# First loads of layer 0 in four pieces, and 79 expert blocks instead of 80, in a two-layer transformer kernel

## The chip, the cores and the metric

One core of a Trainium2 chip runs the whole program. The metric is the device time of one execution in microseconds (us). All data are float32, apart from a few constants and parked values in bfloat16.

## What is computed

Two layers work on x, 2048 tokens of 512 features, in sequences as each step takes them. Every step is added to x and followed by a layer norm:

```python
x = _layernorm(x + _L0_attn_ref(...))    # linear attention, 16 heads of 128, 4 key/value heads, rope, elu + 1
x = _layernorm(x + _L0_xattn_ref(...))   # mLSTM with the context, 16 heads of 32
x = _layernorm(x + _L0_ffn_ref(...))     # silu, silu, rows added by a top-2 router
x = _layernorm(x + _L1_attn_ref(...))    # lightning attention
x = _layernorm(x + _L1_xattn_ref(...))   # softmax attention with the context
x = _layernorm(x + _L1_ffn_ref(...))     # mixture of experts
```

The two places of the change are the first step and the last. The first begins with `k = x @ Wk.T`, with Wk of 512 x 512. The last sends each token to 4 of 16 experts, chosen inside the best 2 of 4 groups; an expert is `silu(x @ W1.T) * (x @ W3.T) @ W2.T` with 352 inner features, its result is weighted by the router's score, and a shared expert with 704 inner features takes every token.

## The kernel before, in words

The program is written engine by engine: SP issues loads and stores, PE multiplies, DVE and ACT evict PSUM banks and do the element-wise work, POOL adds, and issues the indirect transfers. Semaphores (`wait_ge`, `then_inc`) tie them together. Three parts follow each other: `build_layer0` (tiles named a_), `build_layer1` (c_) and `build_experts` (d_).

**Layer 0** takes the 2048 tokens in four groups of 512 (`stages`). A written list (`order`) assigns the products of a group to the 8 PSUM banks in turn: `Tiles.start` lets PE wait until the bank's earlier tile is drained, `Tiles.done` announces the new one. A group begins with four key tiles (L761, `keys`), one for each key head, 128 x 512, each the sum over four 128-row chunks `c` of the features: `w[:, c, ...]` by `xT[:, c, :]`. A float32 product of one chunk stands in the profile as two MATMUL records. Four value tiles follow, then the query tiles of the first heads, then scores. Weights come through a ring of two 1 MB buffers (`ring`, filled by `fill` at L404 in the order of `RING`): keys in buffer 0, values in 1, first queries in 0 again. For the rope DVE makes two partial products of each key or query tile (L994, L997), POOL adds them (L507), ACT takes the exponential (L545, L547), and DVE writes the feature (L1007). The partial buffers are double, so tile n waits for tile n - 2.

At the start SP issues, in this order, xT of group 0 (1 MB, L410), the key weights (1 MB, L404), cos, sin and the identity (64 KB each, L423) and the value weights (L404). ACT's queue carries nine smaller loads beside them (L533, L535). Before its first product PE waits at L733 for cos, sin and the identity together (`weights`, 48) and for nine constants that POOL writes.

**The experts.** A first phase transposes x, runs the router, ranks the chosen pairs, gives each expert as many blocks of 128 rows as it needs, and scatters the token numbers into a slot list in memory (64 indirect DMAs of POOL, L2246), while PE works on the shared expert for groups 0 and 1 (L2336, L2349). The number of blocks is fixed when the program is built: `BLOCKS = TOKENS * TOPK // P + NE`, 64 + 16 = 80. Blocks past the last needed one run with the last expert on rows that nobody reads.

The loop (`Fori(0, BLOCKS // 2)`, two blocks in each turn, buffers v = 0 and 1) runs on every engine. For block j, PE transposes the gathered rows of block j + 1 (`turn`, L2385), makes the gate products of j (`up_rows`, L2395), transposes the hidden rows of j - 1 (`turn_hidden`, L2390), makes the up products of j (L2395) and the down products of j - 1 (`down`, L2402). DVE copies the transposed rows (L2593), the transposed hidden rows (L2596) and multiplies gate by up (L2612); ACT takes silu of the gate (L2323) and copies the down result (L2316); SP stores it (L2219) and fetches the next expert's weights when the owner changes; POOL gathers the rows of j + 1 (L2258). `filled` counts five steps of PE for each block. Behind the loop the down products of the last block are made and stored, then the shared expert runs on groups 2 and 3, while POOL fetches the result rows back (L2274) and DVE adds them, weighted, to y.

## Time and profile before

| | us |
|---|---|
| median of three timed runs | 2944.35 |
| lowest, highest | 2939.48, 2947.29 |
| the profiled execution | 2941.02 |
| its span | 2939.2 |
| PE busy in the span | 2685.3 (91%) |
| DVE, ACT, POOL busy | 1372.6, 839.4, 588.4 |

The span goes from the first to the last instruction that the profiler recorded; the 1.8 us between it and the execution's time lie around it. All rows below are from this one execution. Times in them are counted from the start of the span. PE stands for TensorE's matmuls, PEld for its weight loads, DVE for VectorE, ACT for ScalarE, POOL for GpSimd and SP for SyncE; L745 is line 745 of the kernel, and where a helper issues the instruction it is the helper's line. "issue" is idle time for which the profile shows no releaser.

### The profile page before, as it was taken

The page shows a single profiled execution, that of the slowest core. Times are in us where ns is not written, and L with a number is a line of the kernel's source. Part 1 is how long each engine was busy: PE and PEld are TensorE (multiplying, and loading weights), DVE is VectorE, ACT ScalarE, POOL GpSimd, SP SyncE. Part 2 cuts the span into 40 slices and gives each one's busy share as a digit, 9 for nine tenths or more (in the row PEclk, how much of TensorE's full clock was granted, in tenths as well). Part 3 has the DMA queues.
Part 4 walks back from the last instruction along what each step waited for, and adds up shares of the span by engine and source line. Part 5 has one row for each costly group of instructions (what it writes and reads, how often), then busy time and mean ns, then how long its engine had stood idle before and what let it go on. Part 6 is the DMA issues. An engine that isn't in the chain of part 4 may idle for free. (4 is left out here: it accounts for less than half of the span.)

```text
span 2939.2 us, 33813 instructions
## 1 busy us (share of the span) xinstructions
PE 2685.3 (91%) x10989; PEld 1366.4 (46%) x10990; DVE 1372.6 (47%) x2541; ACT 839.4 (29%) x1894; POOL 588.4 (20%) x632
## 2 busy tenths in 40 slices
PE   7998999999999856799999999769599999999998
PEld 3544554554455342344334433153256555666543
DVE  3555554563557263467777777423012222222255
ACT  2324332432343231145545555510001111111101
POOL 2111101110111000322333223004311111111154
PEclk9999999999999878899999999969699999999999
DMA  5120122122102103435545454240113333342144
GB/s 189 58 72 29 58 72 86 58 83 76 57 29 72 43 1 127 76 72 116 101 106 111 108 105 102 61 163 1 35 57 129 129 128 130 105 154 97 63 140 154
DMA packets 110236, 261.00 MB, mean 89 GB/s; under 512 B 21955, under 2 KB 55619, under 8 KB 98211
## 3 DMA queue, kind: packets, MB, share of 16 engines
q1 hardware_dynamic: 95202, 220.27, 25.3%
q0 software_dynamic: 13648, 38.06, 4.4%
q8 instruction: 71, 1.16, 0.2%
q10 hardware_dynamic: 1264, 1.10, 0.1%
q14 instruction: 51, 0.41, 0.1%
HBM read 203.76 MB, written 55.22 MB: 88 GB/s over the span
## 5 line engine op out<-in xcount | busy, mean ns | idle before, releaser
L2395 PE MATMUL d_bank<-d_w,d_xcol 128*128 x1280 | 407.0, 461 | 0.0
L1957 DVE TENSOR_REDUCE c_mx<-c_pair 128x2 f32<-128x1024 f32 x256 | 303.6, 1217 | 110.5 <-PE c_pair L1818 109.5
L1668 ACT ACTIVATE c_probs<-c_exp 128x512 f32<-128x512 f32 x512 | 277.9, 597 | 218.4 <-PE c_exp L1832 215.3
L745 PE MATMUL a_bank<-a_xT,a_ring 128*128 128x512 f32 x640 | 287.3, 600 | 11.2 <-DMA a_ident<-in_ident 11.2
L507 POOL TENSOR_TENSOR a_ry<-a_rt 128x512 f32<-128x512 f32 x80 | 131.4, 1642 | 790.9 <-DVE a_rt L997 790.9
L2395 PEld LDWEIGHTS d_bank<-d_w,d_xcol 128*128 128x128 f32 x1280 | 231.8, 191 | 102.4 <-issue 1.5
L2402 PE MATMUL d_bank<-d_w,d_hid 128*128 (+1 forms) x486 | 221.9, 592 | 0.6 <-DVE d_hid L2596 0.6
L745 PE MATMUL a_bank<-a_wo,a_ot 128*128 128x512 f32 x512 | 222.4, 592 | 0.0
L2336 PE MATMUL d_bank<-d_xT,d_ws 128*128 128x512 f32 (+1 forms) x384 | 179.4, 620 | 34.9 <-issue 34.2
L745 PEld LDWEIGHTS a_bank<-a_xT,a_ring 128*128 128x128 f32 x640 | 120.8, 193 | 150.6 <-issue 137.2
L1832 PE MATMUL c_exp<-c_qs,c_ks 128*128 128x512 bf16 x512 | 160.3, 384 | 16.0 <-ACT c_probs L1668 7.6
L2316 ACT ACTIVATE d_yrow<-d_bank 128x512 f32<-128x512 f32 x81 | 48.4, 597 | 384.8 <-PE d_bank L2402 384.8
L745 PEld LDWEIGHTS a_bank<-a_wo,a_ot 128*128 128x128 f32 x512 | 97.2, 190 | 121.1 <-issue 120.6
L1818 PE MATMUL c_pair<-c_ks,c_qs 96*128 96x512 bf16 x512 | 144.4, 387 | 3.1 <-DVE c_mx L1957 2.9
L2593 DVE COPY d_xcol<-d_bank 128x512 f32<-128x512 f32 x81 | 56.0, 692 | 194.1 <-PE d_bank L2385 194.1
L1842 PE MATMUL c_pv<-c_probs,c_vt 128*32 128x512 f32 x1024 | 137.3, 608 | 1.0 <-ACT c_probs L1668 1.0
L2336 PEld LDWEIGHTS d_bank<-d_xT,d_ws 128*128 128x128 f32 (+1 forms) x384 | 71.9, 189 | 140.6 <-issue 139.0
L545 ACT ACTIVATE a_ee<-a_ry 128x512 f32<-128x512 f32 x80 | 50.4, 630 | 302.4 <-POOL a_ry L507 302.2
L2402 PEld LDWEIGHTS d_bank<-d_w,d_hid 128*128 128x128 f32 x486 | 92.3, 190 | 95.3 <-issue 77.5
L2596 DVE COPY d_hid<-d_bank 128x384 f32<-128x384 f32 x81 | 45.2, 558 | 164.5 <-PE d_bank L2390 162.5
L2255 POOL COPY d_index<-d_tokens 128x1 uint32 (+1 forms) x81 | 14.9, 184 | 525.1 <-DVE d_xcol L2593 475.2
L994 DVE TENSOR_TENSOR a_rt<-a_bank,a_cos 128x512 f32<-128x512 f32 x80 | 55.0, 687 | 127.3 <-PE a_bank L745 127.2
(299 smaller groups left out, 3765.5 us busy)
## 6 DMA issues: line engine op xcount, KB each, us to landing
d_w<-in_w SPq DMA_DIRECT2D x16, 1408.0 KB
scratch_results<-d_yrow SPq DMA_DIRECT2D x81, 256.0 KB
a_ring<-in_wq SPq DMA_DIRECT2D x16, 1024.0 KB, 4.8
a_wo<-in_wo SPq DMA_DIRECT2D x16, 1024.0 KB, 4.8
c_ks<-scratch_kpark SPq DMA_DIRECT2D x96, 128.0 KB, 4.4
c_qs<-scratch_qpark SPq DMA_DIRECT2D x96, 128.0 KB, 4.4
d_w<-in_w SPq DMA_DIRECT2D x16, 768.0 KB
a_ring<-in_w SPq DMA_DIRECT2D x8, 1024.0 KB, 8.4
```

The source lines that it names most:

```text
L507: pool.tensor_tensor(ry[:, n % 2, :], rt1[:, n % 2, :], rt2[:, n % 2, :], ALU.add).then_inc(rope_sum.sem, 1)
L745: ins = pe.matmul(bank[:, :], lhs(c), rhs(c), start=(c == 0), stop=(c == n - 1))
L994: dve.tensor_tensor(rt1[:, u, :].rearrange("p (b s) -> p b s", b=GB), view, by_batch(cos[:, :]), ALU.mult)
L1668: act.activation(probs[:, (LC * CH * n + k) % RING, :], bank[:, :], ACT.Exp, scale=float(CD) ** -0.5).then_inc(exped.sem, 1)
L1818: ins = pe.matmul(bank[:, 512 * i:512 * i + 512], qs[0:TR, n % STACKS, h, at0:at0 + P], ks[0:TR, n % STACKS, h, :], start=True, stop=True)
L1832: exps.done(pe.matmul(bank[:, :], ks[:, n % STACKS, h, l * P:(l + 1) * P], qs[:, n % STACKS, h, :], start=True, stop=True))
L1842: ins = pe.matmul(pv[32 * j:32 * j + 32, :], head_values(n, q, l, j), probs[:, (LC * CH * n + QUAD * m + j) % RING, :], start=(l == 0), st ...
L1957: dve.tensor_reduce(mx[:, n % 2, at0:at0 + 2], bank[:, :].rearrange("p (i n) -> p i n", i=2), AX.X, ALU.max).then_inc(maxed.sem, 1)
L2336: ins = pe.matmul(bank[0:m, :], w[:, c, c0:c0 + m], xT[:, c, GT * group:GT * (group + 1)], start=(c == 0), stop=(c == KC - 1))
L2395: ins = pe.matmul(bank[:, 0:FI], xcol[:, v, k, :], w13[:, bass.ds(at, 1), which, k, :].rearrange("p a n -> p (a n)"), start=(k == 0), stop ...
L2402: ins = pe.matmul(bank[:, :], hid[:, v, c * P:(c + 1) * P], w2[:, bass.ds(at, 1), c, :].rearrange("p a n -> p (a n)"), start=(c == 0), sto ...
L2593: dve.tensor_copy(xcol[:, v].rearrange("p c n -> p (c n)"), turned_bank[:, :]).then_inc(xcol_ready.sem, 1)
```

## The change

In layer 0 the loads of xT and of the key weights for group 0 are cut into four pieces each, one for each feature chunk, issued in pairs; each pair counts on a semaphore of its own (`chunk_in`). The four key tiles of group 0 are started together, and PE goes through them chunk by chunk: chunk 0 of all four tiles, then chunk 1, and so on. The waits for cos, sin, the identity and the constants now stand behind these products. The ring's counts are adapted, since the first key weights no longer count on the ring's semaphore.

In the experts BLOCKS is 79. The loop runs 39 turns, and block 78 is written out behind it on every engine, without the transpose of rows for a successor; the gate products of that block count two steps on `filled` in its place. The tail behind uses the other buffer. The list of slots and the result tensor shrink by one block. The loads of x into y count on the `chunk_in` semaphores, so that four semaphores of the experts fall away.

```diff
-            return n % 2, n // 2 + 1
+            return n % 2, n // 2 + n % 2
...
-            features(0)
-            fill(("k", 0))
+            for c in range(KC):
+                sp.dma_start(xT[:, c, :], t["xT"][0][:, c, :]).then_inc(chunk_in[c], 16)
+                sp.dma_start(ring[:, 0, c, :], t["wk0"][:, c, :]).then_inc(chunk_in[c], 16)
             for dst, src in ((cos, "cos0"), (sin, "sin0"), (ident, "ident")):
                 sp.dma_start(dst[:], t[src]).then_inc(weights.sem, 16)
             fill(("v", 0))
...
         def _(pe):
+            def first_keys():
+
+                all_banks = tiles.start_together(pe, 0, [("k", 0, j) for j in range(KV0)])
+                for c in range(KC):
+                    pe.wait_ge(chunk_in[c], 32)
+                    for j in range(KV0):
+                        ins = pe.matmul(all_banks[j][:, :], ring[:, 0, c, j * P:(j + 1) * P], xT[:, c, :],
+                                        start=(c == 0), stop=(c == KC - 1))
+                        if c == KC - 1:
+                            tiles.done(ins)
+
+            first_keys()
             pe.wait_ge(weights.sem, 16 * NW)
             pe.wait_ge(consts.sem, 9)
...
                 def keys(js):
-                    if a is None:
-                        return
-                    xT_in.wait(pe, a, 1)
+                    if not a:
+                        return
+                    xT_in.wait(pe, a, 0)
...
-        BLOCKS = TOKENS * TOPK // P + NE
+        BLOCKS = TOKENS * TOPK // P + NE - 1
...
             with sp.Fori(0, BLOCKS // 2) as i:
                 for v in range(2):
...
+                    store_and_fetch(2 * i + v, v)
+            store_and_fetch(BLOCKS - 1, 0)
             sp.wait_ge(yrow_ready.sem, AHEAD + 1 + BLOCKS)
-            sp.dma_start(t["results"][BLOCKS], yrow[:, 0]).then_inc(row_stored[0].sem, 16)
+            sp.dma_start(t["results"][BLOCKS], yrow[:, 1]).then_inc(row_stored[1].sem, 16)
...
             with act.Fori(0, BLOCKS // 2) as i:
                 for v in range(2):
...
-            rows_out(0, BLOCKS // 2, 5 * BLOCKS + 7)
+                    gate_and_rows(2 * i + v, i, v)
+            gate_and_rows(BLOCKS - 1, BLOCKS // 2, 0)
+            rows_out(1, BLOCKS // 2, 5 * BLOCKS + 7)
...
+            def products(j, i, v, more):
+                expert = load_number(pe, owner_no, j + 1)
+                last_at = load_number(pe, owner_no, j) % 2
+
+                if more:
                     pe.wait_ge(gathered[1 - v].sem, 16 * (i + 1 + v))
                     pe.wait_ge(xcol_ready.sem, AHEAD + j + 1)
                     turn(1 - v)
...
+                up_rows(gate_banks[v], v, 0, expert % 2, 1 if more else 2)
...
+            with pe.Fori(0, BLOCKS // 2) as i:
+                for v in range(2):
+                    products(2 * i + v, i, v, True)
+            products(BLOCKS - 1, BLOCKS // 2, 0, False)
             pe.wait_ge(hrow_ready.sem, AHEAD + BLOCKS)
             pe.wait_ge(hid_ready.sem, AHEAD + BLOCKS)
-            turn_hidden(1)
+            turn_hidden(0)
             pe.wait_ge(hid_ready.sem, AHEAD + 1 + BLOCKS)
             pe.wait_ge(yrow_ready.sem, AHEAD + BLOCKS - 1)
-            down(down_banks[0], 1, (NE - 1) % 2)
+            down(down_banks[1], 0, (NE - 1) % 2)
             pe.wait_ge(yrow_ready.sem, AHEAD + BLOCKS + 1)
-            pe.wait_ge(xcol_ready.sem, AHEAD + BLOCKS + 1)
+            pe.wait_ge(xcol_ready.sem, AHEAD + BLOCKS)
...
-                    dve.wait_ge(filled.sem, turned(j + 1))
-                    columns(1 - v)
...
+                    rows_of_block(2 * i + v, v, True)
+            rows_of_block(BLOCKS - 1, 0, False)
```

How the instructions stand on PE at the very start of the program (a_bank0 to a_bank3 hold the four key tiles, the brackets name the semaphores waited for), before:

```order
L745 MATMUL a_bank0<-a_xT,a_ring 128x512 [waits a_xT_in,a_ring_in0,a_consts,a_weights]
L745 MATMUL a_bank0<-a_xT,a_ring 128x512 x3
L745 MATMUL a_bank1<-a_xT,a_ring 128x512 x4
L745 MATMUL a_bank2<-a_xT,a_ring 128x512 x4
L745 MATMUL a_bank3<-a_xT,a_ring 128x512 [waits a_ring_in0,a_xT_in]
L745 MATMUL a_bank3<-a_xT,a_ring 128x512 x3
L745 MATMUL a_bank4<-a_ring,a_xT 128x512 [waits a_ring_in1]
```

and in the change, up to the second chunk and from the last one on:

```order
L742 MATMUL a_bank0<-a_xT,a_ring 128x512 [waits chunk_in0]
L742 MATMUL a_bank1<-a_xT,a_ring 128x512
L742 MATMUL a_bank2<-a_xT,a_ring 128x512
L742 MATMUL a_bank3<-a_xT,a_ring 128x512
L742 MATMUL a_bank0<-a_xT,a_ring 128x512 [waits chunk_in1]
...
L742 MATMUL a_bank0<-a_xT,a_ring 128x512 [waits chunk_in3]
L742 MATMUL a_bank1<-a_xT,a_ring 128x512
L742 MATMUL a_bank2<-a_xT,a_ring 128x512
L742 MATMUL a_bank3<-a_xT,a_ring 128x512
L758 MATMUL a_bank4<-a_ring,a_xT 128x512 [waits a_ring_in1,a_consts,a_weights]
```

The number of products is the same, 16; the waits for the constants moved behind them, to the first value tile.

On SP at the start, before:

```order
L410 DMA a_xT<-in_xT 128x2048
L404 DMA a_ring<-in_wk0 128x2048
L423 DMA a_cos<-in_cos0 128x128
L423 DMA a_sin<-in_sin0 128x128
L423 DMA a_ident<-in_ident 128x128
L404 DMA a_ring<-in_wv0 128x2048
```

and in the change (the pair of the first two rows stands four times):

```order
L421 DMA a_xT<-in_xT 128x512
L422 DMA a_ring<-in_wk0 128x512
...
L424 DMA a_cos<-in_cos0 128x128
L424 DMA a_sin<-in_sin0 128x128
L424 DMA a_ident<-in_ident 128x128
L404 DMA a_ring<-in_wv0 128x2048
```

Cos, sin, the identity and the value weights moved behind six more issues.

On PE at the end of the expert loop, before:

```order
L2402 MATMUL d_bank<-d_w,d_hid 128x512
L2415 REGISTER_ALU
L2415 COMPARE_AND_BRANCH
L2390 MATMUL d_bank<-d_ident,d_hrow 128x128 x3
L2402 MATMUL d_bank<-d_w,d_hid 128x512 x3
L2336 MATMUL d_bank<-d_xT,d_ws 128x512 x40
```

and in the change (TENSOR_LOAD reads an owner's number into a register):

```order
L2453 COMPARE_AND_BRANCH
L2199 TENSOR_LOAD d_owner_no
...
L2412 MATMUL d_bank<-d_w,d_xcol 128x352
...
L2407 MATMUL d_bank<-d_ident,d_hrow 128x128 x3
...
L2419 MATMUL d_bank<-d_w,d_hid 128x512
L2407 MATMUL d_bank<-d_ident,d_hrow 128x128 x3
L2419 MATMUL d_bank<-d_w,d_hid 128x512 x3
L2353 MATMUL d_bank<-d_xT,d_ws 128x512 x40
```

One block's products, without a transpose of gathered rows (L2385 before), now stand between the branch and the tail.

## Rows read from the trace of the kernel before

**Rows 1.** The page, busy time of each engine and share of the span.
```profile
PE 2685.3 (91%) x10989; PEld 1366.4 (46%) x10990; DVE 1372.6 (47%) x2541; ACT 839.4 (29%) x1894; POOL 588.4 (20%) x632
```

**Rows 2.** Waits of PE: total us, times, longest.
```profile
PE d_bank L2336 <- issue: 34.2, 19, 2.5
...
PE a_bank L781 <- DVE a_qf L1007: 17.8, 4, 6.1
...
PE a_bank L745 <- DMA a_ident<-in_ident: 11.2, 1, 11.2
...
PE a_bank L875 <- issue: 2.7, 1, 2.7
```

**Rows 3.** Timeline of SP, 0 to 25: start, us, instruction.
```profile
0.74 0.39 SPq L410 DMA_DIRECT2D a_xT<-in_xT  x1
1.19 0.42 SPq L404 DMA_DIRECT2D a_ring<-in_wk  x1
...
3.35 0.50 SPq L404 DMA_DIRECT2D a_ring<-in_wv  x1
```

**Rows 4.** DMA issues, 0 to 16: KB, median us from issue to landing.
```profile
a_xT<-in_xT SPq DMA_DIRECT2D x1, 1024.0 KB, 5.1
a_ring<-in_wk SPq DMA_DIRECT2D x1, 1024.0 KB, 7.8
a_ring<-in_wv SPq DMA_DIRECT2D x1, 1024.0 KB, 10.8
```

**Rows 5.** Windows; the last three columns are PE clock, DMA share, GB/s.
```profile
1.60:2.80 1.20, 0.00 (x0) 0.00 (x0) 0.00 (x0) 0.00 (x0) 1.20 (x2) 1.00 0.71 131
2.80:4.00 1.20, 0.00 (x0) 0.00 (x0) 0.00 (x0) 0.00 (x0) 1.20 (x4) 1.00 1.04 422
4.00:5.84 1.84, 0.00 (x0) 0.00 (x0) 0.00 (x0) 0.26 (x1) 1.84 (x5) 1.00 1.00 406
```

**Rows 6.** The page's DMA issues, two groups of 256 KB.
```profile
c_cgr<-in_c SPq DMA_DIRECT2D x16, 256.0 KB, 5.8
...
out_x<-d_y SPq DMA_DIRECT2D x16, 256.0 KB, 2.3
```

**Rows 7.** Windows: length; PE, PEld, DVE, ACT, POOL busy; clock, DMA share, GB/s.
```profile
11.16:17.10 5.94, 5.93 (x8) 2.52 (x9) 0.00 (x0) 0.00 (x0) 0.00 (x0) 1.00 0.50 165
17.10:27.80 10.70, 10.70 (x26) 4.75 (x25) 7.59 (x11) 2.52 (x4) 4.06 (x3) 1.00 0.00 0
```

**Rows 8.** Timeline of DVE: last key tile, first query tile.
```profile
28.03 0.69 DVE L994 TENSOR_TENSOR a_rt<-a_bank,a_cos 128x512 f32<-128x512 f32 x1 [0.62 <-PE a_bank L745]
...
33.33 0.69 DVE L1007 SCALAR_TENSOR_TENSOR a_kf<-a_ry,a_ee 128x512 f32<-128x512 f32 x1 [2.48 <-ACT a_ee L547]
...
45.20 0.69 DVE L994 TENSOR_TENSOR a_rt<-a_bank,a_cos 128x512 f32<-128x512 f32 x1 [11.18 <-PE a_bank L745]
```

**Rows 9.** Expert loop: a window of 73 blocks, and PE in the last block.
```profile
2200.00:2789.43 589.43, 589.43 (x2117) 353.91 (x2116) 129.46 (x219) 77.46 (x146) 83.29 (x144) 1.00 0.34 117
...
2789.43 0.60 PE L2385 MATMUL d_bank<-d_ident,d_xrow 128*128 128x128 f32 x4
...
2789.87 2.53 PE L2395 MATMUL d_bank<-d_w,d_xcol 128*128 x8
```

**Rows 10.** Timeline of PE behind the loop.
```profile
2798.65 2.84 PE L2402 MATMUL d_bank<-d_w,d_hid 128*128 128x512 f32 x6 [0.65 <-DVE d_hid L2596]
...
2802.18 1.12 PE L2336 MATMUL d_bank<-d_xT,d_ws 128*128 128x512 f32 x2 [0.69 <-ACT d_yrow L2316]
```

**Rows 11.** Windows in the early shared expert; then all DMA queues, 2036 to 2102.
```profile
2036.00:2050.76 14.76, 14.76 (x35) 6.46 (x34) 0.69 (x1) 0.00 (x0) 11.31 (x12) 1.00 0.02 0
2050.76:2102.35 51.59, 17.37 (x18) 5.06 (x18) 0.69 (x1) 0.60 (x1) 32.99 (x36) 0.54 0.15 49
...
q1 hardware_dynamic: 430, 2.26, 9.2%
q0 software_dynamic: 1546, 0.28, 2.6%
```

More of the change, by code:

```diff
@@ L143, in wait, with build_layer0 @@
         return self.bank(key)
-def build_layer0(nc, t):
+def build_layer0(nc, t, chunk_in):
     with ExitStack() as ctx:
@@ L2107, in build_experts @@
         stats, mom, rstd = sb("stats", [P, SEQS, 6]), sb("mom", [P, SEQS, 2]), sb("rstd", [P, SEQS])
-        loaded = [signal(f"loaded{g}", 0, 16) for g in range(GROUPS)]
         weights, consts, shared_in = signal("weights"), signal("consts"), signal("shared_in")
@@ L2355, in _ @@
                 if b % GB == 0:
[L2356 removed]
+                    pe.wait_ge(chunk_in[b // GB], 32 + 16)
                 bank = first.start(pe, 0, ("xt", b))
@@ L2391, in turn_hidden, with up_rows @@
                 ins.then_inc(filled.sem, 1)
-            def up_rows(bank, v, which, at):
+            def up_rows(bank, v, which, at, steps=1):
                 for k in range(KC):
@@ L2414, in _ @@
             pe.wait_ge(owners.sem, 1)
-            with pe.Fori(0, BLOCKS // 2) as i:
-                for v in range(2):
-                    j = 2 * i + v
-                    expert = load_number(pe, owner_no, j + 1)
-                    last_at = load_number(pe, owner_no, j) % 2
+            def products(j, i, v, more):
+                expert = load_number(pe, owner_no, j + 1)
+                last_at = load_number(pe, owner_no, j) % 2
+                if more:
                     pe.wait_ge(gathered[1 - v].sem, 16 * (i + 1 + v))
@@ L2672, in build_program, with build_layers @@
                ("ovpark", [2, P, 2, D], F32), ("dnpark", [2, 4, 2 * D], F32),
-               ("slots", [P, SEQS * 4 + NE + 2], U32), ("results", [SEQS * 4 + NE + 1, P, D], F32))
+               ("slots", [P, SEQS * 4 + NE + 1], U32), ("results", [SEQS * 4 + NE, P, D], F32))
     for name, shape, dt in scratch:
         t[name] = nc.dram_tensor("scratch_" + name, shape, dt, kind="Internal").ap()
-    build_layer0(nc, t)
+    with ExitStack() as ctx:
+        chunk_in = [ctx.enter_context(nc.semaphore(f"chunk_in{n}")) for n in range(GROUPS)]
+        build_layers(nc, t, chunk_in)
+def build_layers(nc, t, chunk_in):
+    build_layer0(nc, t, chunk_in)
     build_layer1(nc, t)
-    build_experts(nc, t)
+    build_experts(nc, t, chunk_in)
 def chunks_of(n):
@@ L2728, in constants @@
     t["steps_of"] = np.broadcast_to(P * np.arange(1, SEQS, dtype=f), (P, SEQS - 1)).copy()
-    t["block_no"] = np.arange(-1, SEQS * 4 + NE, dtype=f)[None, :].copy()
+    t["block_no"] = np.arange(-1, SEQS * 4 + NE - 1, dtype=f)[None, :].copy()
     seq = np.arange(SEQS)[None, :]
```

73 lines of the change are left out of this document (37 added, 36 removed).

## The prediction

> **What bounds the kernel now.** I read the page first: PE is busy for 91% of the span [rows 1], so what PE does not wait for is free, and what shortens PE's own chain is worth its full length. Then the list of waits, for PE alone [rows 2]. Two of its entries lie where the diff is. PE waits 11.2 us, once, before its first matmul, and what it waits for is the identity matrix, the last of five loads. In the expert loop no wait of PE is listed at all: the end of the loop is set by PE's own work. A third entry matters only as a danger: 34.2 us in 19 pieces that the profile puts down to "issue", in the expert stage ahead of the loop.
>
> **Part one, the start.** SP issues xT, wk, cos, sin, the identity and wv in this order, about 0.45 us apart [rows 3]. xT (1 MB) lands 5.1 us after its issue at 0.74, so at 5.84; wk lands at 1.19 + 7.8 = 8.99, wv at 3.35 + 10.8 = 14.15 [rows 4]. The first keys need xT and wk alone, but PE starts at 11.16. The change lets it start once one quarter of each has landed.
>
> When is that? No row shows such a pair of 256 KB loads at the start, so I bound it. The two groups of 256 KB loads in the page take 2.3 and 5.8 us (medians) from issue to landing [rows 6]; counted from the second issue at 1.19 this gives 3.5 and 7.0. The nearest rows are those of xT itself: the engines moved 0.157 MB from 1.6 to 2.8 us, 0.506 MB in the next 1.2 us and 0.747 MB up to 5.84 [rows 5], together 1.41 MB, of which xT was 1.05 MB, or 74%. At the same share a pair of 0.52 MB is through when 0.70 MB are, at 2.8 + 0.55/0.422 = 4.1. The second issue comes 0.45 us later than that of xT, so I take 4.5: PE starts 11.16 - 4.5 = **6.6 us** earlier, with 7.7 and 4.2 as ends.
>
> The Trainium skill (DMA: Bandwidth & Descriptors, Anatomy of one DMA) gives a fit for one DMA of the software path, about 2.0 us plus the bytes at 436 GB/s. As an estimate from that page the second quarter would land at 1.19 + 2.0 + 0.6 = 3.8 and the gain would be 7.4 instead of 6.6, a sum of 15.9 instead of 15.1; xT by the same fit would take 4.4 us where the row says 5.1, so I stay with the rows.
>
> Does the start stay ahead? The keys are 32 matmul instructions, 8 for each quarter. In the 5.94 us after PE's start the first 7 of them end, one each 0.85 us; the other 25 take 10.70 us, one each 0.43 us [rows 7]. The first rate is half of the second, PE's 1.2 GHz level after standing idle; the column of the granted clock begins later and does not show it. I take the same slow stretch behind the new start. The first quarter then lasts 8 instructions, to about 4.5 + 6.4 = 10.9, when even the whole of wk was in before; the remaining quarters are not waited for. The keys end at 4.5 + 5.94 + 10.70 = 21.1 instead of 27.8.
>
> What else moves: SP has six more loads to issue, 6 x 0.45 = 2.7 us, so identity and wv land by about 13.9 and 16.9. PE now waits for them behind the keys, at 21.1: 4 us of cover, and nothing to pay. The fill of the first query weights waits for the last key tile and moves forward with it.
>
> The four key tiles end together instead of one each 3.4 us. The last of them is finished 6 us earlier, but the first ends at about the 26th instruction, at 4.5 + 5.94 + 19 x 0.43 = 18.6, no earlier than before. DVE's work on one tile is 0.69 + 1.39 + 0.69 = 2.8 us, so its rope of the four keys runs from 18.6 to about 34, as it did: before, the last key product (L1007) was at 33.33 [rows 8]. DVE then stood idle for 11.18 us until the first query tile, at 45.20 [rows 8]. That tile now comes at 38.6, still after 34. So the crowding is paid out of DVE's idle time, and the wait of 6.1 us for the first group's queries [rows 2] starts and ends 6.6 us earlier. If that cover were gone, each us of delay on DVE would come back at that wait.
>
> **Part two, the experts.** The loop runs 80 blocks, 39 turns of two plus one written out make 79. One block is 589.43/73 = 8.07 us of PE, without a gap, measured over 73 blocks [rows 9]. The written-out block also has no transpose of gathered rows for a successor, so one more of these goes: 2789.87 - 2789.43 = 0.44 us [rows 9]. Together **8.5 us**. The gathers of POOL (two fewer), DVE's copies, ACT's two activations and one 256 KB store per block all run beside PE; their going is worth nothing. Behind the loop stands the same tail with the other buffer: the last hidden copy, the last down product, ACT's copy, with idle times of 0.65 and 0.69 us [rows 10], and the shared expert for the last two groups. I leave it unchanged. The code behind the loop is longer; entering it costs nothing in my sum. Its bound is the longest single "issue" idle of PE in layer 0, 2.7 us [rows 2].
>
> **The sum.** 6.6 + 8.1 + 0.4 = 15.1 us. Against the profiled execution, 2941.02 us with its span of 2939.2, this gives 2925.9. That execution lies below the median of 2944.35; the three timed ones and it average 2943.0, and from there I forecast **2928 us**. Differences below 0.3%, 9 us here, can't be told from no change.
>
> **The rivals.**
>
> *The pieces land late* (10%). Eight loads that share the engines with ACT's nine may all come in together, near 8.99, when wk did as a whole. For it: the engines are already at 406 to 422 GB/s from 2.8 us on [rows 5], so splitting adds no bandwidth, only order. Against it: xT, issued first, landed 3.15 us before wk. The start then gives 2.2, the sum is 10.7, the time 2932.
>
> *DVE eats the start's gain* (5%). If the rope of four keys at once ran over into the queries, the wait for the queries would grow by what the start gave. Against it: 4 us of slack between 34 and 38.6. Only the loop's 8.5 would be left: 2934.5.
>
> *The block comes back behind the loop* (6%). The written-out block needs two number loads and fresh code; if PE stood there as long as the block in the loop had cost, the start alone would remain: 2943.0 - 6.6 = 2936.4. Against it: between blocks in the loop the same loads cost PE nothing.
>
> *The starved stretch grows* (5%); this one ends slower. From 2050.76 to 2102.35 PE ran only 18 matmuls where 120 would fit at 0.43 us, while in 2036 to 2102 no instruction queue moved a packet and POOL's software queue carried its scatters into the slot list [rows 11]. I read it as PE out of instructions. The change shifts PE's instruction stream by two waits and drops a few operations elsewhere. Should PE run dry earlier, each us of the earlier stretch loses 1 - 18/120 = 0.85 us; from 18 us earlier on (before 2033) the whole gain is gone, and 30 us earlier gives 2928 + 25 = 2953. Against it: scatters and PE move together, and two instructions are under 0.5 us. The Trainium skill (Runtime: NRT & Kernel Launch, Instruction fetch mechanics) says engines refill in blocks of 256 instructions and that crossing a boundary is mostly hidden; by that there would be no such stretch, and these rows speak against it.
>
> **How the numbers follow.** The forecast has 74%. Its own bounds: start 4.2 to 7.7, loop exit up to 2.7 lost, and 4 us to either side, half of the 7.8 us between the runs of before, for the places where PE's clock falls after a wait at another moment. That is 2943.0 - 16.2 - 4 = 2923 to 2943.0 - 10.0 + 4 = 2937. I open it to 2921 below, since the bounds of the start are medians; 2937 takes in three of the rivals. Faster by over 0.3% means below 2935.5: nearly all of the forecast, most of the late pieces, half of the DVE case, 0.84. Within 0.3%: the loop exit and the rest of these, 0.11. Slower: 0.05.
>
> **What would show it.** Right: the first matmul at 4 to 5 us, released by a landing; no wait inside the keys; the first scores at about 55 instead of 61.5; 79 x 16 = 1264 up-product records instead of 1280; the period still 8.07 us; from the end of the early shared expert to the start of the late one 8.5 us less. Wrong: a first matmul after 7 us, a wait of PE at a later quarter, a first scores matmul that moved less than the first key did, an idle time of PE at the loop's exit, or a starved stretch of another length than 51.6 us. What would make the prediction wrong most easily is that last one, because nothing in the diff sets it and its cause is only read from the rows.

## The result, and the profile after

| us | before | changed |
|---|---|---|
| median, runs side by side on one chip | 2941.91 (10 runs) | 2927.94 (10 runs) |
| lowest, highest | 2936.94, 2951.22 | 2923.89, 2935.62 |
| the profiled execution, its span | 2941.02, 2939.2 | 2924.07, 2922.3 |

The changed kernel takes 0.9946 of the time, 95% interval 0.9935 to 0.9957: 15.9 us less, 12.6 to 19.1. The medians themselves lie 14.0 us apart. The forecast was 2928. Between the profiled executions lie 16.9 us of span, and below I ask where each of them is. In the third group of experiments further down one execution of the kernel before took 10228.68 us; it stands in that group's median of 2897.46 and is left out of the ratios.

The page of the changed kernel, against [rows 1]:

```profile
PE 2666.2 (91%) x10897; PEld 1357.4 (46%) x10957; DVE 1367.9 (47%) x2537; ACT 837.2 (29%) x1892; POOL 585.2 (20%) x628
```

PE is busy for 19.1 us less, but most of that is not work that went. In layer 1 one group of products, 512 instructions in both programs, has only 453 records in the trace of the changed kernel:

```profile
L1832 PE MATMUL c_exp<-c_qs,c_ks 128*128 128x512 bf16 x512 | 160.3, 384 | 16.0 <-ACT c_probs L1668 7.6
```

```profile
L1845 PE MATMUL c_exp<-c_qs,c_ks 128*128 128x512 bf16 x453 | 146.7, 382 | 22.3 <-ACT c_probs L1681 8.2
```

The weight loads of this group number 512 in both, so 59 matmul records are missing, with 13.6 us of busy time. The busy sum can't be used as the measure of the change; the times between events below can. PE's waits, against [rows 2]; L742 is the first key product now, L2353 was L2336, L794 was L781:

```profile
PE d_bank L2353 <- issue: 34.9, 20, 3.2
...
PE a_bank L794 <- DVE a_qf L1020: 17.8, 4, 6.1
...
PE a_bank L742 <- DMA a_ring<-in_wk: 6.4, 1, 6.4
```

The wait at the start went from 11.2 to 6.4 us and has another releaser: the key weights' first piece, no longer the identity. The other two entries are nearly as they were.

PE's timeline at the start (start, us, instruction, idle time before):

```profile
6.45 16.73 PE L742 MATMUL a_bank<-a_xT,a_ring 128*128 128x512 f32 x32 [6.45 <-DMA a_ring<-in_wk]
...
56.73 1.22 PE L794 MATMUL a_bank<-a_qf,a_kf 128*128 128x512 f32 x1 [6.08 <-DVE a_qf L1020]
```

All 32 instructions of the keys are one group without idle time, so no later piece is waited for, although the last piece of the key weights lands only at 5.94 + 7.9 = 13.8, later than the whole load did before (8.99). But the first one starts at 6.45, not 4.5. The first scores start at 56.73 where the kernel before had 61.54 with the same idle time of 6.08: 4.8 us earlier, as much as PE's start, 11.16 - 6.45 = 4.7.

SP's timeline and the DMA issues up to 16 us (KB, median us to landing), against [rows 3, 4]:

```profile
1.18 0.42 SPq L422 DMA_DIRECT2D a_ring<-in_wk  x1
1.65 0.42 SPq L421 DMA_DIRECT2D a_xT<-in_xT  x1
2.12 0.89 SPq L422 DMA_DIRECT2D a_ring<-in_wk  x1
...
4.58 1.31 SPq L421 DMA_DIRECT2D a_xT<-in_xT  x1
...
8.18 0.44 SPq L404 DMA_DIRECT2D a_ring<-in_wv  x1
```

```profile
a_xT<-in_xT SPq DMA_DIRECT2D x4, 256.0 KB, 6.6
a_ring<-in_wk SPq DMA_DIRECT2D x4, 256.0 KB, 7.2
a_ring<-in_wv SPq DMA_DIRECT2D x1, 1024.0 KB, 10.4
```

The second piece of the key weights was issued at 1.18 and released PE 5.3 us later. The fourth, fifth and seventh issue take SP 0.89, 0.89 and 1.31 us instead of 0.42, so the value weights were issued at 8.18 instead of 3.35 and landed at 18.6, by when PE was still in the keys, which end at 23.0.

Windows of the start, against [rows 5] (PEclk, DMA share, GB/s last):

```profile
1.60:2.80 1.20, 0.00 (x0) 0.00 (x0) 0.00 (x0) 0.00 (x0) 1.20 (x2) 1.00 0.63 130
2.80:4.00 1.20, 0.00 (x0) 0.00 (x0) 0.00 (x0) 0.00 (x0) 1.20 (x4) 1.00 0.82 152
4.00:5.84 1.84, 0.00 (x0) 0.00 (x0) 0.00 (x0) 0.00 (x0) 1.84 (x5) 1.00 0.91 289
```

Here is the miss. From 2.8 to 4.0 us the engines moved 152 GB/s where the whole loads gave 422, and 289 instead of 406 after that. They are not idle (share 0.82 and 0.91); they move less in the same time. The figure for 2.8 to 4.0 us varies: the six traces of this start with ACT's nine loads beside it have 146 to 189 GB/s there, and 272 to 289 in the next window; the three traces with whole loads have 377 to 422 and 406 to 417. The same 2 KB rows move 1.4 to 2 times as much in the second window as in the first, so the length of the rows is not all that sets the rate.

DVE's timeline around the keys' end, against [rows 8]; L1007 and L1020 were L994 and L1007:

```profile
20.75 0.69 DVE L1007 TENSOR_TENSOR a_rt<-a_bank,a_cos 128x512 f32<-128x512 f32 x1 [20.75 <-PE a_bank L742]
...
34.30 0.69 DVE L1020 SCALAR_TENSOR_TENSOR a_kf<-a_ry,a_ee 128x512 f32<-128x512 f32 x1 [0.81 <-ACT a_ee L548]
40.39 0.69 DVE L1007 TENSOR_TENSOR a_rt<-a_bank,a_cos 128x512 f32<-128x512 f32 x1 [5.40 <-PE a_bank L758]
```

The rope of the four keys ends 1.0 us later than before, and the first query tile comes 4.8 us earlier. DVE's idle time of 11.18 us shrank to 5.40 and none of the start's gain was lost to it.

A window inside the loop, and PE's timeline at its exit, against [rows 9, 10]; L2412 was L2395, L2407 was L2390, L2419 was L2402:

```profile
2200.00:2770.00 570.00, 570.00 (x2049) 342.57 (x2048) 125.44 (x212) 75.03 (x142) 79.81 (x138) 1.00 0.33 116
```

```profile
2770.36 2.74 PE L2419 MATMUL d_bank<-d_w,d_hid 128*128 x6
2772.93 2.53 PE L2412 MATMUL d_bank<-d_w,d_xcol 128*128 x8
2775.30 0.49 PE L2407 MATMUL d_bank<-d_ident,d_hrow 128*128 128x128 f32 x3
2775.62 2.53 PE L2412 MATMUL d_bank<-d_w,d_xcol 128*128 x8
2777.99 2.74 PE L2419 MATMUL d_bank<-d_w,d_hid 128*128 x6
2780.57 0.49 PE L2407 MATMUL d_bank<-d_ident,d_hrow 128*128 128x128 f32 x3
2781.71 2.84 PE L2419 MATMUL d_bank<-d_w,d_hid 128*128 128x512 f32 x6 [0.65 <-DVE d_hid L2616]
2785.24 1.98 PE L2353 MATMUL d_bank<-d_xT,d_ws 128*128 128x512 f32 x4 [0.69 <-ACT d_yrow L2330]
```

The last of the 39 turns ends with the down products at 2770.36; the written-out block follows at 2772.93 without idle time and without the transpose of rows, and behind it stand the same two idle times of 0.65 and 0.69 us. The page counts 1264 up-product records. From ACT's second gate activation to its first one of the late shared expert it was 643.44 us before and is 634.93: 8.51 less.

The stretch with few matmuls, against [rows 11]:

```profile
2026.24:2041.02 14.78, 14.78 (x35) 6.46 (x34) 0.69 (x1) 0.00 (x0) 11.18 (x12) 1.00 0.02 0
2041.02:2094.33 53.31, 18.38 (x21) 5.26 (x19) 0.69 (x1) 0.60 (x1) 33.73 (x36) 0.55 0.14 48
```

It starts 9.7 us earlier, where the first scatter comes 8.9 earlier, and lasts 53.3 us instead of 51.6.

**The balance of the span.** Followed by ACT's instructions, the changed kernel is 4.8 us ahead from 42 us on, 4.9 at 1200 and 5.5 at 1800. Between 1840 and 1970 the lead grows to 9.4, is 8.4 at the loop's start, stays there through the loop, and is 16.9 at the end. So 4.8 are the start, 8.5 the block, and 3.6 belong to neither part. Most of them arise around the end of layer 1, where PE works in short bursts and the granted clock falls and rises (before, it was 0.74 from 1840 to 1860 us and 1.00 in the next 20). Groups of PE's instructions of before in 1840 to 1975, and of the changed kernel in 1835 to 1966:

```profile
L2364 PE MATMUL d_bank<-d_wg,d_xT 128*128 128x16 f32 x128 | 26.1, 362 | 1.2 <-ACT d_xT L2283 1.2
...
L2359 PE MATMUL d_bank<-d_ident,d_y 128*128 128x128 f32 x64 | 10.1, 338 | 28.5 <-DMA d_y<-scratch_x 28.5
```

```profile
L2381 PE MATMUL d_bank<-d_wg,d_xT 128*128 128x16 f32 x128 | 23.9, 344 | 1.2 <-ACT d_xT L2297 1.2
...
L2376 PE MATMUL d_bank<-d_ident,d_y 128*128 128x128 f32 x64 | 9.3, 319 | 28.8 <-DMA d_y<-scratch_x 28.8
```

The same 128 router products cost 2.2 us less, and the same 64 transposes 0.8: a difference of how fast the same work ran, not of what was to be done.

### The profile page after: what moved, and what is told of

It is laid out like the page before. It is cut to its first block and busy times, and to the rows that moved or that the text cites. A ratio compares the mean times of both kernels' runs of the same rounds, so it can differ in the third digit from the quotient of the medians.

```text
span 2922.3 us, 33609 instructions
## 1 busy us (share of the span) xinstructions
PE 2666.2 (91%) x10897; PEld 1357.4 (46%) x10957; DVE 1367.9 (47%) x2537; ACT 837.2 (29%) x1892; POOL 585.2 (20%) x628
## 3 DMA queue, kind: packets, MB, share of 16 engines
q10 hardware_dynamic: 1264, 1.10, 0.1%
## 5 line engine op out<-in xcount | busy, mean ns | idle before, releaser
L2412 PE MATMUL d_bank<-d_w,d_xcol 128*128 x1264 | 401.8, 461 | 0.0
L2412 PEld LDWEIGHTS d_bank<-d_w,d_xcol 128*128 128x128 f32 x1264 | 228.8, 191 | 101.5 <-issue 1.7
L758 PE MATMUL a_bank<-a_xT,a_ring 128*128 128x512 f32 x608 | 270.5, 596 | 0.0
L2419 PE MATMUL d_bank<-d_w,d_hid 128*128 x480 | 219.1, 592 | 0.7 <-DVE d_hid L2616 0.7
L2353 PE MATMUL d_bank<-d_xT,d_ws 128*128 128x512 f32 (+1 forms) x384 | 180.4, 622 | 35.6 <-issue 34.9
L758 PEld LDWEIGHTS a_bank<-a_xT,a_ring 128*128 128x128 f32 x608 | 113.7, 191 | 130.8 <-issue 128.3
L1845 PE MATMUL c_exp<-c_qs,c_ks 128*128 128x512 bf16 x453 | 146.7, 382 | 22.3 <-ACT c_probs L1681 8.2
L2353 PEld LDWEIGHTS d_bank<-d_xT,d_ws 128*128 128x128 f32 (+1 forms) x384 | 72.1, 189 | 142.0 <-issue 140.4
L2419 PEld LDWEIGHTS d_bank<-d_w,d_hid 128*128 128x128 f32 x480 | 91.1, 190 | 94.1 <-issue 76.5
L1845 PEld LDWEIGHTS c_exp<-c_qs,c_ks 128*128 128x128 bf16 x512 | 46.0, 99 | 144.0 <-issue 70.2
```

Source lines behind the costliest of these rows:

```text
L758: ins = pe.matmul(bank[:, :], lhs(c), rhs(c), start=(c == 0), stop=(c == n - 1))
L1845: exps.done(pe.matmul(bank[:, :], ks[:, n % STACKS, h, l * P:(l + 1) * P], qs[:, n % STACKS, h, :], start=True, stop=True))
L2353: ins = pe.matmul(bank[0:m, :], w[:, c, c0:c0 + m], xT[:, c, GT * group:GT * (group + 1)], start=(c == 0), stop=(c == KC - 1))
L2412: ins = pe.matmul(bank[:, 0:FI], xcol[:, v, k, :], w13[:, bass.ds(at, 1), which, k, :].rearrange("p a n -> p (a n)"), start=(k == 0), stop ...
L2419: ins = pe.matmul(bank[:, :], hid[:, v, c * P:(c + 1) * P], w2[:, bass.ds(at, 1), c, :].rearrange("p a n -> p (a n)"), start=(c == 0), sto ...
```

## The experiments

The kernels ran in three groups of four, each beside the kernel before on one chip. The kernel before had a median of 2942.96 us beside the first four, 2895.86 beside the second, 2897.46 beside the third: the second and third group ran on other chips, and why the level is 47 us lower there is a question of its own, taken up last. Where the expectations of e5_late and e8_two speak of theory A, it is that other loads on the same engines (ACT's nine, and SP's own later pieces) take the first pair's share; theory B is that the pieces themselves move more slowly, because each of the 128 rows is only 2 KB long instead of 8 KB. Every run that shortens the rows also makes the loads smaller, so these two are not told apart.

### One part of the change at a time

**e1_front** has the new start and 80 blocks. (Its text is that of the changed kernel with BLOCKS and the experts as before.)

```diff
-        BLOCKS = TOKENS * TOPK // P + NE - 1
+        BLOCKS = TOKENS * TOPK // P + NE
```

> The first keys alone, with 80 blocks in the loop. Theory (two independent parts): the first matmul starts at about 6.4 us and the first scores about 4.7 us earlier than before; the time is 4.7 us below before, ratio 0.9984. Rival (the start's gain grows downstream, because later waits and clock falls also shrink): 6 to 8 us below before. Other rival (the gain is lost again at a later wait): within 1 us of before.

Measured: 2938.61 us, ratio 0.9987 (0.9974 to 1.0); the first matmul at 6.50, released by the key weights; 643.45 us from the second gate to the late shared expert.

**e2_blocks** is the reverse, the start of before and 79 blocks, with the loop's exit as in the changed kernel.

```diff
-        BLOCKS = TOKENS * TOPK // P + NE
+        BLOCKS = TOKENS * TOPK // P + NE - 1
```

> 79 blocks alone, with the first loads whole and the first matmul at 11.2 us. Theory: one block of 8.07 us and one transpose of gathered rows of 0.44 us go, so 8.5 us below before, ratio 0.9971, and the stretch from the first block to the shared expert behind the loop is 8.5 us shorter. Rival (the two parts are not independent, or leaving the loop costs something): less than 7 us.

Measured: 2933.48 us, ratio 0.9967 (0.9951 to 0.9982); the first matmul at 11.27; 634.93 us from gate to late shared expert.

At their own places in the traces the start is worth 4.7 us (first matmul) and the block 8.5, 0.9984 and 0.9971 of the time; the timed ratios hold both, though that of the start reaches up to 1.0 and doesn't show the gain by itself. The product, 0.9987 x 0.9967 = 0.9954, lies inside the interval of the whole change. So the parts add within these intervals, each some 0.003 wide; in the traces each has the same size alone as together. Over a whole trace a gain of this size can't be followed: the first scores of e1_front came at 56.09, 5.5 us before those of the kernel before, and its span of 2941.6 is still 2.4 us longer.

**e6_81** is the changed kernel with two blocks more (the loop runs 40 turns, one block is still written out behind it).

```diff
-        BLOCKS = TOKENS * TOPK // P + NE - 1
+        BLOCKS = TOKENS * TOPK // P + NE + 1
```

> The changed kernel with 81 blocks instead of 79: one more turn of the loop, the written-out block behind it kept. Theory (each block costs 8.07 us of PE wherever it stands): 2 x 8.07 = 16.1 us above the changed kernel, so 16.1 - 4.7 - 8.5 = 2.9 us above before, ratio 1.001. Rival (the written-out block is dearer or cheaper than one in the loop, and the gain of 8.5 came from elsewhere): another difference than 16.1 to the changed kernel in the stretch from the first block to the tail.

Measured: 2945.55 us, ratio 1.0015 (1.0005 to 1.0025). From gate to late shared expert 651.08 us, which is 16.15 more than with 79 blocks, 2 x 8.07, and 7.64 more than before, 8.07 - 0.44. So the block's price is linear in their number, and writing the last one out costs nothing but gains the 0.44 of the missing transpose.

### What the start waits for

**e3_whole** is the kernel before, with 80 blocks and whole loads, and only moves PE's wait for cos, sin, the identity and the constants behind the keys of group 0.

```diff
-            pe.wait_ge(weights.sem, 16 * NW)
-            pe.wait_ge(consts.sem, 9)
...
+                if a == 0:
+                    pe.wait_ge(weights.sem, 16 * NW)
+                    pe.wait_ge(consts.sem, 9)
```

> No pieces: xT and the key weights stay whole, 80 blocks, keys tile by tile, but PE waits for cos, sin, the identity and the constants behind the keys. Theory A (moving the wait is half of the start's gain): the key weights land at 9.0 us, so the first matmul starts there, 2.2 us earlier than before, and the time is 2.2 us lower. Theory B (splitting is what counts): the same start at 9.0, but splitting gave 4.7, so the pieces are worth 2.5 us more. If the first matmul starts at 11 us, the wait was not what held PE.

```profile
9.20 15.49 PE L742 MATMUL a_bank<-a_xT,a_ring 128*128 128x512 f32 x32 [9.20 <-DMA a_ring<-in_wk]
```

The first matmul comes at 9.20, when the whole of the key weights is in, and 1.96 us before the 11.16 of before. Timed: 2942.28, ratio 0.9996 (0.9984 to 1.0008), which can't be told from no change. Of the 4.7 us at the first matmul, then, 2.0 need no splitting of loads at all, and the splitting brings 2.7. The first scores divide otherwise:

```profile
58.24 4.63 PE L778 MATMUL a_bank<-a_qf,a_kf 128*128 128x512 f32 x5 [6.08 <-DVE a_qf L1007]
```

They come 3.3 us before the 61.54 of before, not 2.0, and only 1.5 after those of the changed kernel. What differs is how long the keys take, from the first of them to the first value product: 15.33 us here, 16.66 before and 16.57 in the changed kernel. PE's first matmuls follow each other at the slow pace of 0.85 us, and the last of them in part; that is 4 of the 32 here, 7 before and 6 in the changed kernel. Nor is this length fixed by the code. In the six traces that have the changed start word for word, the first matmul comes at 6.45 to 6.61, the keys take 15.46 to 16.71 us, and the first scores come at 55.77 to 56.90, 4.6 to 5.8 us before those of the kernel before. With one trace of e3_whole, the pieces' own part at the first scores is 1.3 to 2.5 us and no better known.

**e5_late** lets ACT issue its nine loads only when the first keys' loads are in, so SP's pieces have the engines to themselves.

```diff
+            act.wait_ge(chunk_in[KC - 1], 32)
```

> The changed kernel, but ACT issues its nine late loads only after the fourth pair has landed. It tells why the first pair landed at 6.45 us and not at 4.5. Theory A (ACT's nine loads share the engines and SP's descriptors with the pieces): the first matmul starts 1.5 us or more earlier, at 5 us or below, and SP's later issues take 0.45 us again instead of 0.9 to 1.3. Theory B (2 KB runs move slowly whatever else is there): the first matmul stays within 0.5 us of 6.45 and the engines move about 250 GB/s between 2 and 5 us.

Measured: 2876.91 us in one execution, first matmul at 5.96. **f2_late** is the same kernel, timed beside the changed kernel itself (**f1_changed**):

> The changed kernel itself, once more, as the partner of the next three on one chip. First matmul at 6.0 to 6.6 us, ratio to before 0.9946 as before. Theory 1 (the starved stretch belongs to the chip): it is there or missing in this kernel and in the kernel before alike, with 46 to 51 us lost or with under 5. Theory 2 (it belongs to the kernel's code): it is there in this one, as in its first trace, whatever the chip.

> The changed kernel with ACT's nine loads behind the first keys' loads, timed this time. If the first matmul's 0.6 us is all that they cost, it ends 0.5 to 1 us below the changed kernel, which can't be told from it. If the nine loads also hold up SP (its issues took 0.9 us instead of 0.42), identity and value weights land earlier too, but nobody waits for them, so still no more than 1 us. Over 3 us less would speak against both.

The first matmul of f1_changed came at 6.49, of f2_late at 5.77:

```profile
5.77 16.66 PE L743 MATMUL a_bank<-a_xT,a_ring 128*128 128x512 f32 x32 [5.77 <-DMA a_ring<-in_wk]
```

and the windows of f1_changed from 2.8 us on, then those of f2_late, are:

```profile
2.80:4.00 1.20, 0.00 (x0) 0.00 (x0) 0.00 (x0) 0.00 (x0) 1.20 (x4) 1.00 0.71 189
4.00:5.84 1.84, 0.00 (x0) 0.00 (x0) 0.00 (x0) 0.00 (x0) 1.84 (x5) 1.00 0.93 273
```

```profile
1.60:2.80 1.20, 0.00 (x0) 0.00 (x0) 0.00 (x0) 0.00 (x0) 1.20 (x2) 1.00 0.69 123
2.80:4.00 1.20, 0.00 (x0) 0.00 (x0) 0.00 (x0) 0.00 (x0) 1.20 (x4) 1.00 0.89 186
4.00:5.84 1.84, 0.07 (x1) 0.07 (x1) 0.00 (x0) 0.00 (x0) 1.84 (x5) 1.00 0.89 302
```

The nine loads cost the first pair 0.7 us (0.5 in e5_late) of the 1.95 by which it missed 4.5. SP issues its first six in at most 0.43 us each again, so the long issues of the changed kernel go with ACT's loads, but they were behind the first pair; the seventh still takes 0.76. With nothing beside them the pieces move 186 and 302 GB/s, where f1_changed on the same chip moved 189 and 273: the total stays, and SP gets all of it. Up to 5.84 us SP's queue has moved 0.93 MB in f2_late and 0.58 in f1_changed. So theory A carries about a third of the miss, and not the rate. Timed, f1_changed has 2885.36 us, ratio 0.9961 (0.9946 to 0.9976), and f2_late 2881.84, ratio 0.9951 (0.9937 to 0.9965). The medians are 3.5 us apart, more than the 1 us that I expected and over the 3 that I had said would speak against both readings; the profiled executions differ the other way (spans 2875.3 and 2879.8), and the intervals overlap. It isn't decided that f2_late is faster.

**e8_two** makes two pairs of 512 KB with rows of 4 KB; PE waits at every second chunk.

```diff
-            for c in range(KC):
-                sp.dma_start(xT[:, c, :], t["xT"][0][:, c, :]).then_inc(chunk_in[c], 16)
-                sp.dma_start(ring[:, 0, c, :], t["wk0"][:, c, :]).then_inc(chunk_in[c], 16)
+            for c in (0, 2):
+                sp.dma_start(xT[:, c:c + 2, :], t["xT"][0][:, c:c + 2, :]).then_inc(chunk_in[c], 16)
+                sp.dma_start(ring[:, 0, c:c + 2, :], t["wk0"][:, c:c + 2, :]).then_inc(chunk_in[c], 16)
+                sp.sem_inc(chunk_in[c + 1], 32)
...
-                    pe.wait_ge(chunk_in[c], 32)
+                    pe.wait_ge(chunk_in[c - c % 2], 32)
```

> The changed kernel with two pairs of 512 KB in runs of 4 KB instead of four of 256 KB in runs of 2 KB, ACT's nine loads beside them as before. Theory A (sharing with ACT's loads): twice the bytes at the same share of the engines, the first matmul at 7.5 to 9 us. Theory B (the length of the runs): 4 KB runs move at over 400 GB/s, so the first half lands at about 2.8 + (1.05/0.74 - 0.16)/0.42 = 5.8 us, earlier than the quarter did.

```profile
8.40 15.95 PE L743 MATMUL a_bank<-a_xT,a_ring 128*128 128x512 f32 x32 [8.40 <-DMA a_ring<-in_wk]
```

Measured: 2888.68 us in one execution, the first matmul at 8.40. That lies where theory A put it (7.5 to 9) and far from theory B's 5.8. In the three windows of the start it moved 188, 263 and 265 GB/s. From 2.8 to 4.0 us the rate rises with the row, 152 with 2 KB (189 at most in the other traces), 263 with 4 KB, 422 with 8 KB; but in the next window the 4 KB rows fall behind both others. Theory B has the direction of the first rate and not its size, and misses the landing: halving the number of pieces costs 1.95 us at the first matmul against the changed kernel and gains 0.8 against the whole loads of e3_whole.

Packets add what neither theory had. The queues up to PE's first matmul, or in the kernel before up to the landing of xT: packets, MB, share of 16 engines; q1 carries SP's loads, q10 ACT's. Before, 0 to 5.84:

```profile
q1 hardware_dynamic: 175, 1.30, 61.7%
q10 hardware_dynamic: 162, 0.11, 5.7%
```

the changed kernel, 0 to 6.45:

```profile
q1 hardware_dynamic: 391, 0.73, 45.1%
q10 hardware_dynamic: 346, 0.36, 17.9%
```

and f2_late, 0 to 5.77:

```profile
q1 hardware_dynamic: 486, 0.90, 60.1%
```

In both of the first two kernels the queues move about as many packets as each other, 175 to 162 and 391 to 346; in e8_two it is 417 to 387. What differs is what SP's packets hold, 7.4 KB on average before and 1.9 KB now, so the same give and take hands SP 92% of the bytes before and 67% now. And the number of packets doesn't make up for it: up to the same 5.84 us SP's queue with four times smaller packets moved 299, 1.7 times as many as before. Worked out from the rows above, as an estimate, a packet of SP kept an engine busy for 0.33 us before (61.7% of 16 engines for 5.84 us, over 175) and for 0.12 in the changed kernel (45.1%, 6.45 us, 391), so a packet with a fourth of the bytes took over a third of the time. That the queues take turns by packets is my reading of the counts. SP's loads alone were changed between these three kernels, ACT's never, and where ACT's queue carried pieces of the same size as SP's (e4_act and f3_both, next) the counts were less equal, 255 to 200 and 240 to 187 up to the first matmul.

**e4_act** issues the key weights on ACT, ahead of the nine, and **f3_both** does that and holds the nine back.

```diff
-                sp.dma_start(ring[:, 0, c, :], t["wk0"][:, c, :]).then_inc(chunk_in[c], 16)
...
+            for c in range(KC):
+                act.dma_start(ring[:, 0, c, :], t["wk0"][:, c, :]).then_inc(chunk_in[c], 16)
```

> The changed kernel with the four pieces of the key weights issued by ACT ahead of its nine loads, and the four of xT by SP. Both first pieces are issued at 0.74, and none of the nine competes with the first pair. Theory: the first matmul at about 5 us instead of 6.45. If the landing is set by the 16 engines' rate for 2 KB runs alone, it stays above 6.

> The last one with the key weights issued by ACT, the features by SP, the other nine behind them. If issuing bounds the first pair, it is in at 5.0 to 5.4 us (two queues at once, nothing beside them), 1.2 us before the changed kernel; if the piece size sets the rate, 5.9 to 6.2, as with either edit alone. In time at most 1.5 us below the changed kernel.

```profile
5.96 16.82 PE L744 MATMUL a_bank<-a_xT,a_ring 128*128 128x512 f32 x32 [5.96 <-DMA a_xT<-in_xT]
```

e4_act had its first matmul at 6.21 (one execution, 2880.33 us) where about 5 was expected, f3_both at 5.96, timed 2884.83, ratio 0.9957 (0.9941 to 0.9973). Issuing from two engines buys nothing beyond what holding back the nine does; who issues is not what the first pair waits for.

### The stretch with few matmuls

**e7_drain** lets POOL wait after each 16 of the 64 scatters until they have landed, in case too many outstanding scatters are what starves PE. **f4_drain** is the same kernel again, on the third chip.

```diff
+                pool.wait_ge(list_filled.sem, 16 * SEQS * (k + 1))
```

> The changed kernel, but POOL waits after each 16 of its 64 scatters until they have all landed. It is aimed at the rival that the prediction named for the slower side: the stretch of 52 us in which PE issues one matmul in 2.8 us. Theory A (while the software queue holds unfinished scatters, the engines' instruction fetch does not get through): the queue runs empty three times, a refill slips in, the starved stretch is shorter than 40 us and the time is 10 us or more below the changed kernel. Theory B (something else holds PE, such as POOL's issuing itself): the stretch keeps its 52 us, moved by the few us that the three waits add to the scatters, and the time is within 3 us of the changed kernel.

> POOL waits after each 16 scatters, again. If the stretch is there on this chip and comes from too many scatters outstanding, the matmuls come back between 2040 and 2095 and the time is 20 us or more below the changed kernel. If it comes from something else (code, or scatters as such), the stretch stays, and the time is the changed kernel's, 0 to 4 us above. If the stretch is missing in all kernels here, it is 3 to 4 us above, and the question stays open.

e7_drain: 2886.07 us, ratio 0.9962 (0.9949 to 0.9976). f4_drain: 2888.25, ratio 0.9967 (0.9953 to 0.998). Neither answers its question, because the stretch was there in none of the kernels of the second and third group. f1_changed is the changed kernel word for word; here is the same window of its trace and of the first trace of the changed kernel:

```profile
2040.00:2060.00 20.00, 20.00 (x47) 8.29 (x46) 2.07 (x3) 1.79 (x3) 15.14 (x16) 1.00 0.02 0
```

```profile
2040.00:2060.00 20.00, 6.92 (x10) 1.90 (x8) 0.00 (x0) 0.60 (x1) 15.13 (x16) 0.66 0.02 0
```

POOL issues 16 scatters in both, and PE runs 47 matmuls in the one and 10 in the other. The 292 matmuls of the early shared expert take 173.8 to 176.8 us from the first to the last in six traces, those of the first group and the two first ones, of before and of the changed kernel, and 128.3 to 129.3 in all eight traced on the other two chips. At the end f1_changed is 47.0 us ahead of the first trace of the changed kernel, and that accounts for the lower level of those groups. The kernel before has no trace on the other chips; its time fell by as much. So the stretch belongs neither to the change nor to this kernel's code alone.

The kept traces also say something on the reading of [rows 11], "PE out of instructions". In all 14 of them PE runs 142 to 144 matmuls between one packet of an instruction queue shortly before the stretch and the next one behind it, and no such packet comes between: the two are at 2018 and 2127 us in the kernel before and at 2007 and 2069 in f1_changed. So these packets keep step with PE's own progress, and on the two other chips PE runs through the same instructions at full pace without any. No packet is seen that PE could have been waiting for. This speaks against the reading, and leaves nothing in its place. Whether the stretch comes from the chip itself or from something set up with it (where the program lies in memory, say) wasn't tried; what sets it stays open, and so does whether draining the scatters would help where it is.

Where the stretch is missing, something else bounds the loop's start. PE's timeline in f1_changed:

```profile
2065.25 20.87 PE L2366 MATMUL d_bank<-d_ws,d_hs 128*128 128x512 f32 x48 [0.78 <-DVE d_hs L2539]
2090.69 0.78 PE L2402 MATMUL d_bank<-d_ident,d_xrow 128*128 128x128 f32 x4 [4.57 <-DMA d_xrow<-scratch_x,d_index]
2094.49 1.11 PE L2402 MATMUL d_bank<-d_ident,d_xrow 128*128 128x128 f32 x4 [3.01 <-issue]
```

The early shared expert is done, and PE waits 4.57 us for the first gathered rows, which wait for the slot list, which waits for the last scatter. There the drain's 3.4 us (83.1 us from the first scatter to the last instead of 79.7) lie on the path: from the first scatter to the first transpose of gathered rows it is 94.3 us in f4_drain and 91.0 in f1_changed, and the medians are 2.9 us apart.

## Why the prediction was right, and where it was off

- **Which wait bounds the start**: right. Taking the identity off the path and splitting the loads moved the first matmul by 4.7 us and the first scores by 4.8, so nothing was lost on the way. e3_whole separates the two edits at the first matmul, 2.0 and 2.7 us, which the prediction had not done.
- **The start's size**: this is the term that was mis-sized, 6.6 predicted, 4.7 measured (inside its ends of 7.7 and 4.2). The step that failed is "At the same share a pair of 0.52 MB is through when 0.70 MB are, at 2.8 + 0.55/0.422 = 4.1". It took rate and share from loads with 8 KB rows, and held that splitting "adds no bandwidth, only order"; it took bandwidth away. With pieces the rate was 152 GB/s instead of 422, and SP's part of the bytes 67% up to 6.45 us; SP's queue had moved 0.56 MB, just over the pair's 0.52, by 5.84 instead of 4.1. The row of the small loads that took 5.8 us to land [rows 6], used for the bound only, was the nearer one: it gave 7.0, and the release came at 6.45. The other group of loads of the same size in those rows gave 3.5, so the size alone would not have told which to take.
- **The slow stretch behind the start**: as taken in this trace, and not a constant. The keys lasted 23.02 - 6.45 = 16.57 us, before 27.83 - 11.17 = 16.66; over all traces it is 15.33 to 16.71, and 15.46 to 16.71 with the same code. No quarter was waited for.
- **"SP has six more loads to issue, 6 x 0.45 = 2.7 us"**: wrong in size. The value weights were issued 4.8 us later, since an issue took up to 1.31 us. The cover was there all the same: they landed at 18.6 and were wanted at 23.0.
- **DVE's crowding**: right in kind. The last key product at 34.30 (forecast 34), idle time 5.40 left before the first query tile at 40.39 (forecast 38.6, off by the start's 1.9). The 34 has no working behind it: four tiles at 2.8 us from 18.6 end at 29.8. DVE in fact began at 20.75 and waited for ACT between tiles, so that the end was met is partly luck.
- **The block and the transpose**: right to 0.01 us, 8.51 measured in every kernel with 79 blocks, and linear with 81.
- **The loop's exit**: right, no idle time, the tail's two waits unchanged.
- **The sum**: 15.1 forecast; 4.8 + 8.5 = 13.3 in the traces, which is 0.9955 of the time and inside the intervals of both comparisons of the whole change (0.9935 to 0.9957, 0.9946 to 0.9976). That 2928 was met to 0.1 us is partly luck: the level of 2943.0 that it was counted from was 1.1 above the median measured beside the change, the start gave 1.9 less, and some 3 us of the first comparison come from places where the same work ran faster for no reason in the diff.
- **The rivals**: "The pieces land late" is nearest to what happened; the first pair landed 2 us late, not 4.5, while the last piece of the key weights came later than that rival had it, 13.8 instead of near 8.99, and nobody waited for it. "DVE eats the start's gain" and "The block comes back behind the loop" did not occur (e1_front, e2_blocks). "The starved stretch grows": it grew by 1.7 us in the trace, and it moved with the scatters, as the argument against that rival had it. My reading of it, "PE out of instructions", has the packets of the instruction queues against it, and what holds PE there stays open. The Trainium skill (Runtime: NRT & Kernel Launch, Instruction fetch mechanics) says that crossing a boundary between blocks of instructions is mostly hidden. The prediction took the stretch as evidence against that; since the packets stand at the same place in PE's work with the stretch and without it, the rows are no evidence against that sentence, and no run here tests it.

## What to carry to other kernels

Before splitting a load for an earlier start, look at what else PE waits for: moving a wait for data that the first products don't read gave 2.0 of the 4.7 us at the first matmul here, and 3.3 us at the first scores in its one trace, for three lines. When a load is cut along its rows, don't take the rate of the whole load for the pieces; look for landing times of loads of the piece's own size, take the later ones for the start of a kernel, where 256 KB issued at 1.18 came in 5.3 us later here, and count whose packets share the engines. A loop on the bound engine with a steady period makes a forecast to the hundredth of a us, while places where the clock wavers move the total by several us either way, so check a part's worth between two events close around it, not by the span.

## What the runs showed of the hardware that I had not expected

- Cutting 1 MB loads with 8 KB rows into 256 KB pieces with 2 KB rows brought the traffic between 2.8 and 4.0 us from 377 to 422 GB/s (three traces) down to 146 to 189 (six traces). With ACT's loads held back it was 186 and 193, so those loads take a share and do not set the rate.
- SP's queue and ACT's, with loads at the same time, moved nearly equal numbers of packets (175 to 162, 391 to 346, 417 to 387) while SP's rows had 8, 2 and 4 KB. With 2 KB rows on both, it was 255 to 200 and 240 to 187.
- SP's issue of one load took up to 0.42 us for the first three and, in the first trace of the changed kernel, 0.56 to 1.31 for the next five, while ACT's nine loads were in the queues; with those held back, the first six took 0.43 at most and the seventh 0.76 and 0.79.
- The slow pace with which PE starts after standing idle lasted for 4 to 7 of the 32 key instructions, and the keys took 15.46 to 16.71 us, in traces whose code up to there is the same.
- The kernel before ran in 2943 us on one chip and in 2896 and 2897 on two others. In the changed kernel, which was traced on all three, 46.7 us of that difference lie in one stretch beside POOL's scatters, in which PE ran one matmul each 2.5 us and its granted clock fell to 0.50. No instruction-queue packet came late there; the cause is open.
